# A ternary feed-forward stage and a sparse-expert stage with their element-wise work dealt out anew over VectorE, ScalarE and GpSimd

## The chip, the cores and the metric

One core of one Trainium2 chip runs the whole program in one launch. The metric is device time in microseconds (us), the median of several executions. Five engines take part, each with its own queue of instructions worked off in order: TensorE (PE, and PEld for its weight loads), VectorE (DVE), ScalarE (ACT), GpSimd (POOL) and SyncE (SP), which only issues transfers here. They meet at semaphores: an instruction adds to one when it is done, and another queue waits until the count is reached. While a queue waits, everything behind the waiting instruction waits too.

## The reference, cut to what matters

Two transformer layers over 2048 tokens of width 512. The change touches both feed-forward parts. Layer 0's is ternary, with hidden width 2048:

```python
def bitlinear(x, w):
    xn = layer_norm(x)
    x_hat = clip(xn * 128 / gamma, -128 + eps, 128 - eps) * gamma / 128   # gamma = max|xn| of the row
    w_hat = sign(round(w / (mean|w| + eps))) * mean|w|
    return x_hat @ w_hat.T
h = gelu(bitlinear(x, w_fc))          # 512 -> 2048
y = bitlinear(h, w_proj)              # 2048 -> 512
x = layernorm(x + y)
```

Layer 1's is a mixture of experts: 16 experts of inner width 352, two for each token, and a shared expert:

```python
gu = x @ w_gate_up[e]                 # 512 -> 704
h  = silu(gu[:352]) * gu[352:]
y += combine[t, e] * (h @ w_down[e])  # 352 -> 512
```

## The kernel before

Every fp32 operand of a product goes to TensorE as two f16 numbers: a high part (rounded to f16) and a low part (what the rounding left). A high part is written by ScalarE, a low part by a subtraction after it.

**The order of the work.** In a stage each engine has a list of pairs (lag, function). In step s it calls, in the order of the list, every function with tile t = s - lag. `unrolled` writes all steps out; `run_tiles` writes the first and last steps out and puts the middle into a loop of two steps. So the order of the list is the order in the engine's queue, and the lag says in which step a tile reaches it. Two buffers (t % 2) stand behind nearly every tile.

**The ternary stage** (`ternary_ffn`) goes over 16 tiles of 128 tokens. In a step TensorE does the first product of one tile (`fc`, 32 matmuls in four banks of PSUM), the transposes of the hidden rows of an older one (`ht`, 32 in four turns through two banks), the transposes of a younger one's input (`xt`) and the second product (`proj`, 32 matmuls). ScalarE applies gelu, bank by bank, and writes both high parts (`xhi`, `hhi`). VectorE has the statistics of three normalisations (`bn_stats`), the normalisations themselves (`normalize`), the search for the largest value and the clip (`AbsmaxQuantizer.apply`), and the residual sum. Copies of the transposed hidden rows from PSUM (`evacuate`) are split, two turns to ScalarE and two to VectorE. GpSimd takes roots (`root`) and both low parts (`xlo`, `hlo`).

**The sparse stage** (`sparse_experts`) goes over 48 tiles of 128 token places, each with its expert's weights. For each tile SyncE loads fp32 weights; ScalarE writes their high parts (`gate_hi`, 128x2816; `down_hi`, 128x1024 and 96x512), VectorE the low parts (`gate_lo`, `down_lo`). TensorE does the two halves of the first product (`gate`, `up`), ScalarE a tanh, VectorE two operations to the hidden rows (`swiglu`; its result is `hid`, announced by `h_done`), ScalarE their high part (`hhi`), GpSimd their low part (`hlo`), TensorE the transposes (`tr`), ScalarE their copy (`hevac`), TensorE the second product (`down`), and ScalarE its copy to SBUF (`yevac`). GpSimd also gathers the token rows.

Of the kernel before, what the change touches and what calls it, by code (L numbers as in the profile page):

```python
# [803 lines left out]
def ternary_ffn(nc, m):  # L804


    NB = FF // D
    NK = FF // P
    with Phase(nc, "ffn") as f:
# [24 lines left out]
        with f.block() as block:
            @block.tensor
            def _(pe):
                def xt(t, u):
# [3 lines left out]
                    transpose_parts(pe, ps_x, x2[u], m).then_inc(xt_done, 1)  # L841

                def fc(t, u, banks):
                    pe.wait_ge(xt_evac, t + 1)
                    for n in banks:
                        after(pe, gelu_done, t * NB - (NB - n - 1))
                        for k in range(KC):
                            for part in range(2):
                                last = pe.matmul(ps_fc[n][:, :], xT[u][:, part, k, :],  # L849
                                                 m.wfcT[:, k, n * D:(n + 1) * D],  # L850
                                                 start=(k == 0 and part == 0), stop=(k == KC - 1 and part == 1))
# [2 lines left out]
                def ht(t, u, turns):
                    pe.wait_ge(hh_done, t + 1)
                    pe.wait_ge(hl_done, t + 1)
                    for g in turns:
                        part, k0 = part_of(g)
                        after(pe, (ht_evac_a, ht_evac_d)[g % 2], t * 2 + g // 2)
                        for k in range(8):  # L860
                            last = pe.transpose(ps_h[g % 2][:, k, :],  # L861
                                                h2[u][:, part, (k0 + k) * P:(k0 + k + 1) * P], m.ident16[:, :])
                        last.then_inc(ht_done, 1)

                def proj(t, u):
# [1226 lines left out]
```

## Time and profile before

| | |
|---|---|
| median of 3 runs | 2095.75 us (2095.16 to 2096.2) |
| the profiled execution's own time | 2098.51 us |
| its span | 2096.7 us |
| PE, DVE, ACT, POOL busy, share of the span | 80%, 70%, 48%, 27% |
| mean granted TensorE clock | 0.93 of full speed |
| ternary stage, first and last instruction of VectorE | 774.75 to 1104.4 us |
| sparse stage, first gather to the last copy of a result | 1594.3 to 1975.9 us |

A row of the timeline gives the start of an instruction (or of several merged ones) from the start of the span, its duration, both in us, the engine, the line, what is written and what is read, and in brackets how long its engine sat idle before it and who ended the wait. The distance between two starts on one engine is what an instruction really takes of its queue: it is about 0.1 us shorter than the duration where the next one need not wait for its result. The stages follow each other with a barrier between them, so that time won or lost in one is won or lost for the program unless the next stage has a transfer to wait for.

### The profile page before, as it was taken

How to read it: one execution, taken by the hardware profiler on the slowest of the kernel's cores; microseconds unless marked ns; L12 is line 12 of the kernel's file. 1: busy time of each engine (PE TensorE's matmuls, PEld its weight loads, DVE VectorE, ACT ScalarE, POOL GpSimd, SP SyncE). 2: the span in 40 equal slices, each digit the busy share in tenths (PEclk: the TensorE clock that was granted, in tenths of full speed). 3: DMA queues.
4: the chain of work that ended last, by engine and by line, in shares of the span. 5: the costliest groups of instructions: out<-in, count | busy, mean ns of one | idle time of the engine just before them, and what ended most of it. 6: DMA issues, size and time to landing. Idle time of an engine off the chain costs nothing. (4 is left out here: it accounts for less than half of the span.)

```text
span 2096.7 us, 35409 instructions
## 1 busy us (share of the span) xinstructions
PE 1678.1 (80%) x13401; PEld 864.9 (41%) x13401; DVE 1463.9 (70%) x2115; ACT 997.4 (48%) x1549; POOL 571.1 (27%) x568
## 2 busy tenths in 40 slices
PE   0579999777999858888984977974696888888697
PEld 0353333344333223444441543543463555555364
DVE  3558998446898478999963364364624999999667
ACT  4345777434677713333333222222133777777532
POOL 0250000252000033344321122123261444444255
PEclk9889999998999989999996988996798999999899
DMA  8000000000000000000002000002004665345234
GB/s 298 1 2 2 2 2 2 1 1 1 2 2 2 2 1 1 1 0 0 1 1 91 1 1 1 1 1 96 32 2 144 195 195 153 113 154 183 94 102 139
DMA packets 49393, 105.96 MB, mean 51 GB/s; under 512 B 7096, under 2 KB 10392, under 8 KB 48720
## 3 DMA queue, kind: packets, MB, share of 16 engines
q1 hardware_dynamic: 37632, 75.99, 10.4%
q0 software_dynamic: 7424, 21.00, 3.9%
q10 hardware_dynamic: 4176, 6.82, 0.9%
q8 instruction: 103, 1.69, 0.3%
q14 instruction: 58, 0.48, 0.1%
HBM read 149.68 MB, written 21.01 MB: 81 GB/s over the span
## 5 line engine op out<-in xcount | busy, mean ns | idle before, releaser
L624 ACT ACTIVATE attn_prob<-attn_ps_t 128x512 f32<-128x512 f32 x576 | 312.6, 595 | 127.9 <-PE attn_ps_t L591 126.3
L643 DVE TENSOR_REDUCE attn_mx<-attn_ps_s 128x2 f32<-128x1024 f32 (+3 forms) x304 | 342.8, 1163 | 41.5 <-PE attn_ps_s L572 38.0
L136 PE MATMUL sparse_ps_g<-sparse_wg,sparse_xT 128*128 128x352 f16 x1152 | 190.5, 316 | 54.7 <-DVE sparse_xT L1900 54.7
L604 PE MATMUL attn_ps_o<-attn_prob,V 128*32 128x256 f32 x2304 | 174.8, 389 | 3.6 <-ACT attn_prob L624 2.7
L1905 DVE SCALAR_TENSOR_TENSOR sparse_wg<-sparse_raw_g,sparse_wg 128x2816 f16<-128x2816 f32 x48 | 148.4, 3092 | 37.9 <-ACT sparse_wg L1857 37.8
L136 PEld LDWEIGHTS sparse_ps_g<-sparse_wg,sparse_xT 128*128 128x128 f16 x1152 | 107.8, 99 | 128.8 <-DVE sparse_xT L1900 77.7
L778 POOL TENSOR_TENSOR wo_o<-O,wo_o 128x512 f16<-128x512 f32 (+1 forms) x16 | 18.4, 1153 | 496.0 <-ACT wo_o L750 495.9
L1942 POOL TENSOR_TENSOR sparse_h<-sparse_hid,sparse_h 128x352 f16<-128x352 f32 x48 | 87.7, 1826 | 217.4 <-ACT sparse_h L1876 217.4
L1021 PE MATMUL lin_ps_z<-w,lin_xT 128*128 128x512 f16 x576 | 136.2, 387 | 0.0
L1857 ACT ACTIVATE sparse_wg<-sparse_raw_g 128x2816 f16<-128x2816 f32 x48 | 122.0, 2541 | 17.2 <-DMA sparse_raw_g<-in_L_ffn_w_gate_up_dram 17.2
L849 PE MATMUL ffn_ps_fc<-wfcT,ffn_xT 128*128 128x512 f16 x512 | 123.6, 393 | 8.1 <-DVE ffn_xT L926 8.1
L591 PE MATMUL attn_ps_t<-QT,KT 64*128 64x256 f16 x1152 | 112.3, 273 | 18.6 <-ACT attn_prob L624 11.4
L871 PE MATMUL ffn_ps_y<-wprojT,ffn_hT 128*128 128x512 f16 x512 | 116.2, 386 | 10.6 <-issue 8.8
L572 PE MATMUL attn_ps_s<-KT,QT 64*128 64x512 f16 (+3 forms) x768 | 115.2, 336 | 2.1 <-DVE attn_mx L643 2.1
L1845 PE MATMUL sparse_ps_y<-sparse_wd,sparse_hT 128*128 128x512 f16 (+1 forms) x432 | 102.7, 383 | 1.0 <-ACT sparse_hT L1883 1.0
L908 ACT ACTIVATE ffn_hT<-ffn_ps_h 128x1024 f16<-128x1024 f16 x32 | 32.8, 1024 | 138.2 <-PE ffn_ps_h L861 138.2
L1021 PEld LDWEIGHTS lin_ps_z<-w,lin_xT 128*128 128x128 f16 x576 | 53.3, 99 | 70.3 <-issue 15.6
L591 PEld LDWEIGHTS attn_ps_t<-QT,KT 64*128 64x128 f16 x1152 | 39.0, 94 | 100.0 <-ACT attn_prob L624 45.1
L871 PEld LDWEIGHTS ffn_ps_y<-wprojT,ffn_hT 128*128 128x128 f16 x512 | 50.0, 99 | 71.4 <-issue 14.2
L604 PEld LDWEIGHTS attn_ps_o<-attn_prob,V 128*32 128x32 f32 x2304 | 49.3, 108 | 69.9 <-issue 37.5
L849 PEld LDWEIGHTS ffn_ps_fc<-wfcT,ffn_xT 128*128 128x128 f16 x512 | 49.9, 100 | 65.7 <-DVE ffn_xT L926 8.9
L962 POOL TENSOR_TENSOR ffn_h<-ffn_hn,ffn_h 128x2048 f16<-128x2048 f32 x16 | 65.0, 4065 | 37.4 <-ACT ffn_h L906 37.4
(320 smaller groups left out, 3407.2 us busy)
## 6 DMA issues: line engine op xcount, KB each, us to landing
sparse_raw_g<-in_L_ffn_w_gate_up_dram SPq DMA_DIRECT2D x48, 1408.0 KB
sparse_raw_d<-in_L_ffn_w_down_dram SPq DMA_DIRECT2D x48, 512.0 KB
y_d<-sparse_y SPq DMA_DIRECT2D x48, 256.0 KB, 3.6
sparse_raw_d<-in_L_ffn_w_down_dram SPq DMA_DIRECT2D x48, 192.0 KB
prep_w_fc<-in_L_ffn_w_fc_dram SPq DMA_DIRECT2D x4, 1024.0 KB, 15.6
X<-in_L_attn_x_dram ACTq DMA_DIRECT2D x1, 4096.0 KB, 39.6
prep_w_proj<-in_L_ffn_w_proj_dram SPq DMA_DIRECT2D x4, 1024.0 KB, 22.4
x_d<-route_x SPq DMA_DIRECT2D x16, 256.0 KB, 2.0
```

Of the source, the lines that this page charges most:

```text
L136: last = pe.matmul(out, a(k), b(k), start=(k == 0 and n == 0), stop=(k == chunks - 1 and n == 2))
L572: last = pe.matmul(banks[par][:, h, :], QT[s, pair + h, qt * P:(qt + 1) * P], KT[s, (pair + h) // 2, c * 512:c * 512 + n], start=not diago ...
L591: last = pe.matmul(ps_t[:, (2 * g + par) % 3, i, :], KT[s, j, kt * P:(kt + 1) * P], QT[s, 2 * j:2 * j + 2, qt * P:(qt + 1) * P], start=kt ...
L604: last = pe.matmul(ps_o[32 * jj:32 * jj + 32, 256 * half:256 * half + 256], V[:, kt, 4 * jg + jj, :], prob[(2 * q + jj // 2) % 4][:, half, ...
L624: act.activation(prob[g % 4][:, par, :, :], ps_t[:, (2 * g + par) % 3, :, :], ACT.Exp, scale=HD ** -0.5).then_inc(exp_done, 1)
L643: dve.tensor_reduce(mx[x % 2][:, c, :, at:at + per], ps_s[:, 2 * (r % 2):2 * (r % 2) + 2, 0:per * n].rearrange("p e (h k) -> p e h k", k=n ...
L849: last = pe.matmul(ps_fc[n][:, :], xT[u][:, part, k, :], m.wfcT[:, k, n * D:(n + 1) * D], start=(k == 0 and part == 0), stop=(k == KC - 1 ...
L871: last = pe.matmul(ps_y[:, :], hT[u][:, part, k, :], m.wprojT[:, k, :], start=(k == 0 and part == 0), stop=(k == NK - 1 and part == 1))
L1021: last = pe.matmul(out, xT[:, a, k, :], m.w1[:, b, i, k, :], start=False, stop=(k == KC - 1 and n == 2))
L1845: last = pe.matmul(ps_y[u][:, :], hT[u][0:size, a, k, :], wd[u][0:size, c, k, :], start=(k == 0 and n == 0), stop=(k == 2 and n == 2))
L1857: act.activation(wg[u][:, 0, :, :], raw_g[r][:, :, :], ACT.Copy, scale=WS).then_inc(gh_done, 1)
L1905: dve.scalar_tensor_tensor(wg[u][:, 1, :, :], raw_g[r][:, :, :], WS, wg[u][:, 0, :, :], ALU.mult, ALU.subtract).then_inc(gl_done, 1)
```

## The change

In the ternary stage the loop gives way to steps written out one by one, and the work is dealt out in another way:

- GpSimd keeps the roots, and multiplies the root of the hidden rows by minus their mean (`shift`). Both low parts go to VectorE.
- ScalarE applies the normalisation of the hidden rows (one 128x2048 operation with the root as scale and `shift` as bias) and copies all four turns of transposed rows. VectorE loses these.
- The lags are shorter by one from the hidden normalisation on (`proj` has 6 in place of 7), the lists are in another order, the first transposes of a tile wait for its high part alone, and each half of `proj` waits for its own two turns.

In the sparse stage `hlo` moves from GpSimd to VectorE, between `xevac` and `down_lo`, and on ScalarE `hhi` and `down_hi` change places.

```diff
 @block.tensor                                                    # ternary stage
-                def ht(t, u, turns):
-                    pe.wait_ge(hh_done, t + 1)
-                    pe.wait_ge(hl_done, t + 1)
+                def ht(t, turns):
+                    pe.wait_ge(hh_done, t + 1)
+                    if turns[0] == 2:
+                        pe.wait_ge(hl_done, t + 1)
...
-                    pe.wait_ge(ht_evac_a, t * 2 + 2)
-                    pe.wait_ge(ht_evac_d, t * 2 + 2)
                     for part in range(2):
+                        pe.wait_ge(ht_evac, t * 4 + 2 * part + 2)
...
-                run_tiles(pe, NT, [(4, of(fc, 0)), (7, of(ht, 0, 1)), (4, of(fc, 1, 2)), (7, of(ht, 2, 3)),
-                                   (4, of(fc, 3)), (3, xt), (7, proj)])
+                unrolled(NT, [(4, lambda t: fc(t, (0,))), (6, lambda t: ht(t, (0, 1))), (4, lambda t: fc(t, (1, 2))),
+                              (6, lambda t: ht(t, (2, 3))), (4, lambda t: fc(t, (3,))), (3, xt), (6, proj)])
 @block.scalar
+                def h_norm(t):
+                    u = t % 2
+                    act.wait_ge(shift_done, t + 1)
+                    after(act, hl_done, t - 1)
+                    act.activation(hn[u][:, :], h[u][:, :, :].rearrange("p n k -> p (n k)"), ACT.Identity,
+                                   scale=ln_h.rstd[u][:, :], bias=shift[u][:, :]).then_inc(hn_done, 1)
...
-                run_tiles(act, NT, [(7, evacuate(act, copy, ht_evac_a, 0)), (4, gelu(0, 1)),
-                                    (7, evacuate(act, copy, ht_evac_a, 2)), (4, gelu(2, 3)), (2, xhi), (6, hhi)])
+                unrolled(NT, [(4, gelu(0)), (6, hevac(0, 1)), (5, hhi), (4, gelu(1, 2)), (6, hevac(2, 3)), (4, gelu(3)),
+                              (2, xhi), (4, h_norm)])
 @block.vector
+                    dve.tensor_scalar(back[u][:, :], ln_h.mv[u][:, 0:1], -1.0, None, ALU.mult).then_inc(back_done, 1)
+                def h_clip(t):
+                    dve.wait_ge(hn_done, t + 1)
+                    q_h.apply(dve, hn[t % 2][:, :], t, t % 2)
+                def hlo(t):
+                    u = t % 2
+                    dve.wait_ge(hh_done, t + 1)
+                    after(dve, ht_done, t * 4 - 4)
+                    dve.tensor_tensor(h2[u][:, 1, :], hn[u][:, :], h2[u][:, 0, :], ALU.subtract).then_inc(hl_done, 1)
...
-                run_tiles(dve, NT, [(6, h_norm), (9, norm), (8, residual), (7, turn(1)), (5, h_stats), (7, turn(3)),
-                                    (3, x_evac), (1, x_norm), (0, x_stats)])
+                unrolled(NT, [(5, h_clip), (8, norm), (7, residual), (5, hlo), (1, x_norm), (4, h_stats), (3, x_evac), (2, xlo), (0, x_stats)])
 @block.gpsimd
+                def h_root(t):
+                    u = t % 2
+                    after(pool, hn_done, t - 1)
+                    pool.wait_ge(ln_h.s_var, t + 1)
+                    pool.tensor_tensor(ln_h.rstd[u][:, :], ln_h.var[u][:, :], m.minus_half[:, :], ALU.pow).then_inc(ln_h.s_rstd, 1)
+                    pool.wait_ge(back_done, t + 1)
+                    pool.wait_ge(ln_h.s_rstd, t + 1)
+                    pool.tensor_tensor(shift[u][:, :], back[u][:, :], ln_h.rstd[u][:, :], ALU.mult).then_inc(shift_done, 1)
...
-                run_tiles(pool, NT, [(8, lambda t, u: ln_r.root(pool, t, u)), (5, lambda t, u: ln_h.root(pool, t, u)),
-                                     (6, hlo), (2, xlo), (0, lambda t, u: ln_x.root(pool, t, u))])
+                unrolled(NT, [(7, lambda t: ln_r.root(pool, t, t % 2)), (4, h_root), (0, lambda t: ln_x.root(pool, t, t % 2))])
 sparse stage
-                unrolled(NG, [(1, gate_hi), (2, tanh), (3, hevac), (2, down_hi), (2, hhi), (3, yevac)])
+                unrolled(NG, [(1, gate_hi), (2, tanh), (3, hevac), (2, hhi), (2, down_hi), (3, yevac)])
...
-                unrolled(NG, [(1, gate_lo), (2, swiglu), (1, xevac), (2, down_lo)])
+                unrolled(NG, [(1, gate_lo), (2, swiglu), (1, xevac), (2, hlo), (2, down_lo)])
...
-                unrolled(NG, [(0, gather), (2, hlo)])
+                unrolled(NG, [(0, gather)])
```

Three places show what this does to a queue. The first is ScalarE in the middle of the sparse stage, before the change, from one high part of the hidden rows (`sparse_h`) to the next; `sparse_y` is `yevac`, `sparse_wg` is `gate_hi`, `sparse_th` the tanh, `sparse_hT` is `hevac` and `sparse_wd` is `down_hi`:

```order
L1876 ACTIVATE sparse_h<-sparse_hid 128x352
L1889 ACTIVATE sparse_y<-sparse_ps_y 128x512
L1857 ACTIVATE sparse_wg<-sparse_raw_g 128x2816
L1870 ACTIVATE sparse_th<-sparse_ps_g 128x352
L1882 ACTIVATE sparse_hT<-sparse_ps_h 128x2x256
L1883 ACTIVATE sparse_hT<-sparse_ps_h 96x2x128
L1863 ACTIVATE sparse_wd<-sparse_raw_d 128x1024
L1864 ACTIVATE sparse_wd<-sparse_raw_d 96x512
L1876 ACTIVATE sparse_h<-sparse_hid 128x352
```

And ScalarE at the same place after the change; the lines have other numbers, since functions ahead of them have grown:

```order
L1896 ACTIVATE sparse_h<-sparse_hid 128x352
L1883 ACTIVATE sparse_wd<-sparse_raw_d 128x1024
L1884 ACTIVATE sparse_wd<-sparse_raw_d 96x512
L1909 ACTIVATE sparse_y<-sparse_ps_y 128x512
L1877 ACTIVATE sparse_wg<-sparse_raw_g 128x2816
L1890 ACTIVATE sparse_th<-sparse_ps_g 128x352
L1902 ACTIVATE sparse_hT<-sparse_ps_h 128x2x256
L1903 ACTIVATE sparse_hT<-sparse_ps_h 96x2x128
L1896 ACTIVATE sparse_h<-sparse_hid 128x352
```

`down_hi` stood ahead of the high part of the hidden rows, and now stands between it and `yevac` with the next `gate_hi`.

The second place is VectorE in a full step of the ternary stage, before the change, from the normalisation of the hidden rows (`ffn_hn`) to their statistics:

```order
L717 TENSOR_SCALAR ffn_hn<-ffn_h,ffn_lnh_mv,ffn_lnh_rstd 128x2048
L794 TENSOR_REDUCE ffn_qh_g<-ffn_hn 128x1
L797 TENSOR_SCALAR ffn_qh_limit<-ffn_qh_g 128x1 x2
L800 TENSOR_SCALAR ffn_hn<-ffn_hn,ffn_qh_limit 128x2048
L717 TENSOR_SCALAR X<-ffn_r,ffn_lnr_mv,ffn_lnr_rstd 128x512
L940 SCALAR_TENSOR_TENSOR ffn_r<-ffn_ps_y,gamma,X 128x512
L700 BN_STATS ffn_lnr_stats<-ffn_r 128x6
L703 MEMSET ffn_lnr_pad 128x1
L704 BN_AGGR ffn_lnr_mv<-ffn_lnr_stats 128x2
L706 TENSOR_SCALAR ffn_lnr_var<-ffn_lnr_mv 128x1
L885 COPY ffn_hT<-ffn_ps_h 128x1024
L700 BN_STATS ffn_lnh_stats<-ffn_h 128x6 x4
```

And VectorE after the change, from the search for the largest value (the first operation of `h_clip`) to the normalisation of the next input (`ffn_xn`):

```order
L794 TENSOR_REDUCE ffn_qh_g<-ffn_hn 128x1
L797 TENSOR_SCALAR ffn_qh_limit<-ffn_qh_g 128x1 x2
L800 TENSOR_SCALAR ffn_hn<-ffn_hn,ffn_qh_limit 128x2048
L717 TENSOR_SCALAR X<-ffn_r,ffn_lnr_mv,ffn_lnr_rstd 128x512
L965 SCALAR_TENSOR_TENSOR ffn_r<-ffn_ps_y,gamma,X 128x512
L700 BN_STATS ffn_lnr_stats<-ffn_r 128x6
L703 MEMSET ffn_lnr_pad 128x1
L704 BN_AGGR ffn_lnr_mv<-ffn_lnr_stats 128x2
L706 TENSOR_SCALAR ffn_lnr_var<-ffn_lnr_mv 128x1
L960 TENSOR_TENSOR ffn_h<-ffn_hn,ffn_h 128x2048
L717 TENSOR_SCALAR ffn_xn<-X,ffn_lnx_mv,ffn_lnx_rstd 128x512
```

The normalisation in front is gone, and so is the copy of transposed rows (`ffn_hT`) behind the residual's statistics; in the copy's place stands the low part of the hidden rows (`ffn_h`, a subtraction over 2048 columns), and the statistics of the hidden rows now come after the input's normalisation and clip.

## Rows read from the trace of the kernel before

**Rows 1.** Busy time by engine, granted clock and DMA in the middle of both stages.
```profile
880.00:970.00 90.00, 76.23 (x477) 39.45 (x476) 86.17 (x145) 32.88 (x38) 33.84 (x23) 0.98 0.00 0
1720.00:1820.00 100.00, 85.52 (x616) 50.23 (x615) 93.10 (x82) 78.75 (x107) 40.37 (x27) 1.00 0.45 134
```

**Rows 2.** Timeline of the sparse stage, one tile's round.
```profile
1780.66 0.52 DVE L1915 SCALAR_TENSOR_TENSOR sparse_hid<-sparse_a,sparse_ps_g 128x352 f32<-128x352 f32 x1
...
1781.21 0.50 ACT L1876 ACTIVATE sparse_h<-sparse_hid 128x352 f16<-128x352 f32 x1 [1.58 <-DVE sparse_hid L1915]
...
1781.79 1.84 POOL L1942 TENSOR_TENSOR sparse_h<-sparse_hid,sparse_h 128x352 f16<-128x352 f32 x1 [4.34 <-ACT sparse_h L1876]
...
1782.10 2.54 ACT L1857 ACTIVATE sparse_wg<-sparse_raw_g 128x2816 f16<-128x2816 f32 x1
1782.83 1.34 DVE L1923 SCALAR_TENSOR_TENSOR sparse_wd<-sparse_raw_d,sparse_wd 96x512 f16<-96x512 f32 x1
...
1784.67 3.09 DVE L1905 SCALAR_TENSOR_TENSOR sparse_wg<-sparse_raw_g,sparse_wg 128x2816 f16<-128x2816 f32 x1 [0.49 <-ACT sparse_wg L1857]
...
1785.62 1.06 ACT L1863 ACTIVATE sparse_wd<-sparse_raw_d 128x1024 f16<-128x1024 f32 x1
...
1786.57 0.63 ACT L1864 ACTIVATE sparse_wd<-sparse_raw_d 96x512 f16<-96x512 f32 x1
...
1788.23 0.52 DVE L1915 SCALAR_TENSOR_TENSOR sparse_hid<-sparse_a,sparse_ps_g 128x352 f32<-128x352 f32 x1
```

**Rows 3.** The shape of `down_lo`'s last piece, behind the sparse stage, by shape.
```profile
L1531 DVE SCALAR_TENSOR_TENSOR ws_d<-sparse_raw_d,ws_d 96x512 f16<-96x512 f32 x1 | 0.7, 679 | 0.0
```

**Rows 4.** Timeline of the ternary stage, VectorE and GpSimd.
```profile
942.97 2.46 DVE L700 BATCH_NORM_STATS2 ffn_lnh_stats<-ffn_h 128x6 f32<-128x512 f32 x4
...
945.76 0.15 DVE L706 TENSOR_SCALAR ffn_lnh_var<-ffn_lnh_mv 128x1 f32<-128x1 f32 x1
...
947.07 0.54 DVE L717 TENSOR_SCALAR ffn_xn<-X,ffn_lnx_mv,ffn_lnx_rstd 128x512 f32 x1
...
948.61 4.40 DVE L800 TENSOR_SCALAR ffn_xn<-ffn_xn,ffn_qx_limit 128x512 f32<-128x512 f32 x1
948.66 4.07 POOL L962 TENSOR_TENSOR ffn_h<-ffn_hn,ffn_h 128x2048 f16<-128x2048 f32 x1 [2.11 <-ACT ffn_h L906]
...
955.86 2.29 DVE L794 TENSOR_REDUCE ffn_qh_g<-ffn_hn 128x1 f32<-128x2048 f32 x1
...
959.69 0.54 DVE L717 TENSOR_SCALAR X<-ffn_r,ffn_lnr_mv,ffn_lnr_rstd 128x512 f32 x1
...
961.99 0.69 DVE L885 COPY ffn_hT<-ffn_ps_h 128x1024 f16<-128x1024 f16 x1
```

**Rows 5.** Timeline of the ternary stage, TensorE: first product, one round, last product.
```profile
784.87 8.42 PE L849 MATMUL ffn_ps_fc<-wfcT,ffn_xT 128*128 128x512 f16 x32 [2.34 <-DVE ffn_xT L926]
...
946.65 7.07 PE L871 MATMUL ffn_ps_y<-wprojT,ffn_hT 128*128 128x512 f16 x32 [0.75 <-issue]
...
962.74 0.62 PE L861 MATMUL ffn_ps_h<-ident,ffn_h 128*128 128x128 f16 x8 [2.50 <-DVE ffn_hT L885]
...
966.29 7.07 PE L871 MATMUL ffn_ps_y<-wprojT,ffn_hT 128*128 128x512 f16 x32 [0.75 <-issue]
...
1094.21 7.07 PE L871 MATMUL ffn_ps_y<-wprojT,ffn_hT 128*128 128x512 f16 x32 [0.90 <-ACT ffn_hT L908]
```

**Rows 6.** Groups of like instructions by shape, nearest to those the change adds.
```profile
L906 ACT ACTIVATE ffn_h<-ffn_hn 128x2048 f16<-128x2048 f32 x16 | 30.4, 1900 | 0.0
L908 ACT ACTIVATE ffn_hT<-ffn_ps_h 128x1024 f16<-128x1024 f16 x32 | 32.8, 1024 | 138.2 <-PE ffn_ps_h L861 138.2
L711 POOL TENSOR_TENSOR ffn_lnh_rstd<-ffn_lnh_var,minus_half 128x1 f32<-128x1 f32 x16 | 8.8, 548 | 54.1 <-DVE ffn_lnh_var L706 54.1
L1008 DVE SCALAR_TENSOR_TENSOR w<-linw_rawWqk,w 128x2048 f16<-128x2048 f32 x1 | 2.3, 2293 | 10.5 <-ACT w L1000 10.5
L411 POOL TENSOR_TENSOR qkv_pad<-minus_half 128x1 f32<-128x1 f32 x16 | 3.1, 193 | 1.3
```

More of the change, by code:

```diff
@@ L817, in ternary_ffn @@
         r = [f.sb(f"r{u}", [P, D], F32) for u in range(2)]
+        back = [f.sb(f"back{u}", [P, 1], F32) for u in range(2)]
+        shift = [f.sb(f"shift{u}", [P, 1], F32) for u in range(2)]
+        ps_fc = [f.ps(f"ps_fc{n}", [P, D], F32) for n in range(NB)]
         ps_x = f.ps("ps_x", [P, 2, KC, P], F16)
-        ps_fc = [f.ps(f"ps_fc{n}", [P, D], F32) for n in range(NB)]
         ps_h = [f.ps(f"ps_h{n}", [P, 8, P], F16) for n in range(2)]
@@ L840, in xt, with fc @@
                     after(pe, xt_evac, t)
-                    transpose_parts(pe, ps_x, x2[u], m).then_inc(xt_done, 1)
-                def fc(t, u, banks):
+                    transpose_parts(pe, ps_x, x2[t % 2], m).then_inc(xt_done, 1)
+                def ht(t, turns):
+                    pe.wait_ge(hh_done, t + 1)
+                    if turns[0] == 2:
+                        pe.wait_ge(hl_done, t + 1)
+                    for g in turns:
+                        after(pe, ht_evac, t * 4 + g - 1)
+                        part, k0 = g // 2, (g % 2) * 8
+                        for k in range(8):
+                            last = pe.transpose(ps_h[g % 2][:, k, :],
+                                                h2[t % 2][:, part, (k0 + k) * P:(k0 + k + 1) * P], m.ident16[:, :])
+                        last.then_inc(ht_done, 1)
+                def fc(t, banks):
+                    u = t % 2
                     pe.wait_ge(xt_evac, t + 1)
@@ L848, in fc, with proj @@
                             for part in range(2):
[L849 to L850 removed]
+                                last = pe.matmul(ps_fc[n][:, :], xT[u][:, part, k, :], m.wfcT[:, k, n * D:(n + 1) * D],
                                                  start=(k == 0 and part == 0), stop=(k == KC - 1 and part == 1))
                         last.then_inc(fc_done, 1)
[L854 to L867 removed]
+                def proj(t):
+                    u = t % 2
                     after(pe, r_done, t)
                     for part in range(2):
+                        pe.wait_ge(ht_evac, t * 4 + 2 * part + 2)
                         for k in range(NK):
@@ L908, in _, with hhi @@
-                copy = lambda out, in_: act.activation(out, in_, ACT.Copy)
-                run_tiles(act, NT, [(7, evacuate(act, copy, ht_evac_a, 0)), (4, gelu(0, 1)),
-                                    (7, evacuate(act, copy, ht_evac_a, 2)), (4, gelu(2, 3)), (2, xhi), (6, hhi)])
+                def hhi(t):
+                    u = t % 2
+                    act.wait_ge(q_h.s_clipped, t + 1)
+                    after(act, ht_done, t * 4 - 6)
+                    act.activation(h2[u][:, 0, :], hn[u][:, :], ACT.Copy).then_inc(hh_done, 1)
```

101 lines of the change are left out of this document (46 added, 55 removed).

## The prediction

> **What bounds the kernel now.** I read the busy time by stretch first, to see which engine is full in the two stages, and then one round (one tile's share) of each in the timeline, to see which wait ends last.
>
> In the ternary stage VectorE is busy 86.17 of 90 us and TensorE 76.23 [rows 1]. TensorE waits 2.50 us for VectorE's copy of transposed rows, and 0.75 us more ahead of `proj`; its round is 966.29 - 946.65 = 19.64 us [rows 5]. VectorE sets it, and not by work alone: the clip of the input (128x512) takes 4.40 us, and ends when GpSimd's low part of 4.07 us, begun 0.05 us later, has ended [rows 4]. A normalisation of the same shape takes 0.54 [rows 4], so 3.9 us a round are a lock-out.
>
> In the sparse stage VectorE is busy 93.10 of 100 us, and DMA 0.45 [rows 1]. Here the timeline is needed, for VectorE still waits 0.49 us for ScalarE in every round. The round is a ring through two engines [rows 2]: `hid` starts at 1780.66; ScalarE, idle for 1.58 us, starts the high part 0.55 later; with `yevac` between them `gate_hi` starts 0.89 after that; `gate_lo` 2.57 after it; the next `hid` 3.56 after it. The sum is 7.57 us. Whatever ScalarE does between the wait for `hid` and `gate_hi` lengthens the ring; what it does ahead of the wait is covered by 1.58 us of idleness. `down_hi` is now ahead of it.
>
> **The change, part by part: the sparse stage.** `down_hi` goes behind the high part, into the ring. Its first piece holds ScalarE's queue for 1786.57 - 1785.62 = 0.95 us, its second for about 0.53 (0.63 less the overlap of 0.1) [rows 2]. The ring becomes 7.57 + 1.48 = 9.05 us. What lay under cover ahead of `hid` leaves only more idleness there.
>
> VectorE gains a subtraction over 352 columns, about 0.5 us (its neighbour of that width takes 0.52) [rows 2]. Its input is ready 0.55 + 0.50 us after `hid` starts; VectorE has until then its `hid` and the copy of `xT` (0.69 for that shape [rows 4]), so it hardly waits. VectorE loses a stall: `down_lo`'s last piece takes 1.34 us while GpSimd's low part runs [rows 2], and 0.68 with GpSimd quiet [rows 3]. VectorE's own work was 7.57 - 0.49 = 7.08 and becomes 7.08 - 0.66 + 0.5 = 6.9 us, far under 9.05: nothing is won. `down_lo` waits for `down_hi`, until 2.5 us after `hid`, and is through 1.8 us later, before `gate_lo` may start at 5.5. TensorE has 0.86 x 7.57 = 6.5 us of work [rows 1] and stays covered. The transfers have more time than before.
>
> The ring is closed from tile 0's `hid` to tile 46's: 46 rounds, 46 x 1.48 = 68 us, and about 0.4 at the end, where tile 47's second product waits for `down_lo`. **Sparse stage: +68.5.** Bounds: with the pieces' whole durations, 1.06 + 0.63 = 1.69, it is 78; if the second piece overlapped with its successor as the first does, by 0.11, 67.
>
> **The ternary stage.** GpSimd's two subtractions go, and with them the 3.9 us. I sum VectorE's round after the change from the start of `h_clip` in its new order. Largest value, limits and clip: 959.69 - 955.86 = 3.83; output normalisation, residual and its statistics: 961.99 - 959.69 = 2.30; low part of 2048 columns: 2.2, from the same subtraction of weights at 2.29 less overlap [rows 4, 6]; input normalisation, largest value and clip: 948.61 - 947.07 = 1.54 plus 0.46 for the clip; hidden statistics to the start of the variance: 945.76 - 942.97 = 2.79 [rows 4]. That makes 13.12 us.
>
> Then the root. GpSimd starts 0.25 us after the variance has started and takes 0.55 [rows 6]. The new multiplication (`shift`, 128x1) could start at 0.85. VectorE meanwhile clears the copy of `xT` and starts `xlo` at about 0.8, for 0.68 (the row of this width) [rows 3]. The rows show that such a subtraction and a GpSimd operation exclude each other: GpSimd's 1.84 us began when VectorE's piece ran, VectorE's 1.34 waited for the end of it [rows 2]. So I let the multiplication wait until 1.46 and take 0.2, as a 128x1 operation of 0.193 does [rows 6]. ScalarE's normalisation of 2048 columns takes 1.90, as its high part does [rows 6], and 0.1 goes to signals. `h_clip` can start 3.66 after the variance. **Round: 13.12 + 3.66 = 16.8 us.** Without the collision it is 16.2.
>
> The Trainium skill (SBUF — State Buffer, Who interferes with whom) says the same of the pair: a VectorE instruction with two inputs in SBUF contends with a GpSimd one that reads SBUF, whichever starts first holding it off. It speaks against `xlo` beside `shift`; by it the round is the longer of my two, and the rows of the sparse stage agree (1.34 us against 0.68).
>
> The other engines: TensorE's round is 19.64 - 2.50 - 0.75 = 16.4 us [rows 5], just covered. ScalarE adds 1.90 and two copies of 1.02 [rows 6] to the 32.88 us that it has in 90 [rows 1]: about 11 us, covered as a sum, but in the order of its queue the high part of the hidden rows stands behind two copies. It is ready for it 3.97 us after `h_clip` starts, and VectorE asks for it at 6.13; 1.9 us fit between.
>
> The edges. The copy of the first `xT` now stands behind one more input normalisation and `xlo`, so the first `fc` starts about 2.5 us later than 784.87 [rows 5], at 787.4. It takes 8.4; gelu 0.9; statistics 2.79; to `h_clip` 3.66: 803.1. There the pipe is not yet full, and `h_clip` (3.9), high part (2.0), low part (2.2), input (2.0), statistics (2.79) and root path (3.66) stand in a line: `h_clip` of tile 1 at 819.7. 14 rounds of 16.8 less about 2 for the last three, which have no input work, give 1053 for tile 15. There ScalarE does the copies of tile 14's second half only behind tile 15's high part, at 7.9; half a `proj` later, at 11.4, tile 15's transposes and copies take 3.1 and its `proj` 7.07: end at 1053 + 21.6 = 1074.6, against 1094.21 + 7.07 = 1101.3 [rows 5]. **Ternary stage: -27.** Bounds: a round of 16.2 gives -35; a round of 17.5 (if the low part were 0.3 slower, and half a microsecond went to signals) gives -17. The vanished loop I cost at nothing, for the 0.75 us of TensorE in the round is within the time that it has to spare.
>
> **The sum.** 2098.5 (the profiled execution) + 68.5 - 27 = 2140; the median lies 2.75 lower, so 2137 us.
>
> **The rivals.**
> (1) The forecast: the sparse ring grows by 1.48, the ternary round lies between 16.2 and 17.5. From 2095.75 + 67 - 35 to + 78 - 17: 2128 to 2157. Chance 0.76.
> (2) The ternary stage gains little, because ScalarE becomes the place where it queues: copies wait for TensorE, the high part behind them, and with it VectorE's low part. For: the order of its queue, in which one late copy holds up four functions. Against: 2.2 us of room ahead of the high part. It decides when TensorE's first transposes come more than about 2 us late; a round of 18.5 gives 14 x 1.7 = 24 us back: 2161. Chance 0.11.
> (3) The sparse stage doesn't grow, and the whole is faster: if `gate_hi` were ready well ahead of need, the 1.48 us would fall into idle time, and the ternary gain would stand alone: 2095.75 - 27 = 2069. It takes 1.48 us of slack between `gate_hi`'s end and `gate_lo`. Against: the slack is negative, 0.49 us of waiting in every round, and `gate_lo` starts 0.03 after `gate_hi` has ended [rows 2]. Chance 0.05.
> (4) A mixture near no change: half of the sparse loss (34) and a ternary gain of 35, about 2096. Nothing in the rows would halve the loss. Chance 0.03.
> (5) TensorE, idle longer in the sparse stage, is granted less clock: it has 1.00 there with 0.86 busy and 0.98 in the ternary stage [rows 1]; its share falls to 0.72. Only if its work rose beyond the ring would it count; 0.3 us a round are 14 us: 2151. Chance 0.05, inside the range.
>
> **The numbers.** The likeliest is 2137. Below 2120 lie (3), (4) and an edge of (1), above 2155 lies (2) and a little of (1): 2120 to 2155 leaves out about 0.2. A measurement of this kernel can tell 0.2%, 4.2 us, from no change. Faster by more has (3) and a third of (4): 0.06; within it 0.02; slower 0.92.
>
> **What would show each step.** The sparse rounds at 9.05 us, `down_hi` between the high part and `yevac`, ScalarE's idleness ahead of `hid` up from 1.58 to about 3.1 and VectorE's ahead of `gate_lo` from 0.49 to about 1.3; `down_lo`'s last piece at 0.68. In the ternary stage no 128x512 clip over 0.6, rounds of 16.8, `shift` starting when `xlo` ends, VectorE idle for ScalarE's normalisation about 1.2 us a round. Rounds of 7.6 in the sparse stage would refute the ring; ternary rounds over 17.5 would refute the order that I summed, and a `shift` that starts beside `xlo` the collision.

## The result: 2138.74 us, and the profile after

The changed kernel takes 2138.74 us, the median of four runs (2135.87 to 2142.16); the kernel before took 2095.45 beside it (2093.37 to 2096.2, four runs). The ratio is 1.0209 with an interval of 1.0187 to 1.023: 43.3 us more. The forecast was 2137, with 2120 to 2155 as its range. The profiled execution took 2135.87 us with a span of 2134.1, against 2098.51 and 2096.7 before.

The busy time in the same stretches as in [rows 1] (length; PE, PEld, DVE, ACT and POOL busy; the granted clock; DMA share and GB/s):

```profile
880.00:970.00 90.00, 87.44 (x558) 45.11 (x557) 80.87 (x165) 54.13 (x56) 22.56 (x23) 1.00 0.00 1
1720.00:1820.00 100.00, 73.24 (x518) 43.28 (x519) 77.19 (x79) 66.53 (x90) 37.34 (x11) 1.00 0.38 124
```

The two stages went opposite ways. In the ternary stage TensorE rose from 76.23 to 87.44 of 90 us: the same work is packed closer. In the sparse stage every engine fell, VectorE from 93.10 to 77.19 of 100 and TensorE from 85.52 to 73.24, and so did the DMA: all of them wait.

One round of the sparse stage after the change, from the timeline (start, duration, engine, line, operation, names, and in brackets the idle time before it and what ended it). It answers to [rows 2]:

```profile
1800.72 0.52 DVE L1935 SCALAR_TENSOR_TENSOR sparse_hid<-sparse_a,sparse_ps_g 128x352 f32<-128x352 f32 x1
...
1801.27 0.50 ACT L1896 ACTIVATE sparse_h<-sparse_hid 128x352 f16<-128x352 f32 x1 [3.04 <-DVE sparse_hid L1935]
1801.67 1.04 ACT L1883 ACTIVATE sparse_wd<-sparse_raw_d 128x1024 f16<-128x1024 f32 x1
1801.80 0.53 DVE L1950 TENSOR_TENSOR sparse_h<-sparse_hid,sparse_h 128x352 f16<-128x352 f32 x1
...
1802.62 0.61 ACT L1884 ACTIVATE sparse_wd<-sparse_raw_d 96x512 f16<-96x512 f32 x1
...
1803.14 0.57 ACT L1909 ACTIVATE sparse_y<-sparse_ps_y 128x512 f32<-128x512 f32 x1
1803.26 1.23 DVE L1941 SCALAR_TENSOR_TENSOR sparse_wd<-sparse_raw_d,sparse_wd 128x1024 f16<-128x1024 f32 x1 [0.94 <-ACT sparse_wd L1884]
...
1803.62 2.54 ACT L1877 ACTIVATE sparse_wg<-sparse_raw_g 128x2816 f16<-128x2816 f32 x1
...
1804.41 0.68 DVE L1943 SCALAR_TENSOR_TENSOR sparse_wd<-sparse_raw_d,sparse_wd 96x512 f16<-96x512 f32 x1
...
1806.18 3.09 DVE L1925 SCALAR_TENSOR_TENSOR sparse_wg<-sparse_raw_g,sparse_wg 128x2816 f16<-128x2816 f32 x1 [1.10 <-ACT sparse_wg L1877]
...
1806.70 3.40 POOL L1961 DMA_INDIRECT sparse_xg<-x_d,token  x1 [5.63 <-PE sparse_ps_x L1830]
...
1809.74 0.52 DVE L1935 SCALAR_TENSOR_TENSOR sparse_hid<-sparse_a,sparse_ps_g 128x352 f32<-128x352 f32 x1
```

`hid` to `hid` is 1809.74 - 1800.72 = 9.02 us, where it was 7.57. Follow it with a finger: `hid` ends the 3.04 us wait of ScalarE, the high part starts 0.55 after it, `down_hi` takes 1803.14 - 1801.67 = 1.47, then `yevac` and `gate_hi`, which ends VectorE's wait of 1.10; `gate_lo`, and `hid` again. The waits over 300 us of the stage say the same (waiting engine, tile, line, what it waited for; sum, times, longest):

```profile
ACT sparse_h L1896 <- DVE sparse_hid L1935: 100.4, 33, 3.0
...
DVE sparse_wg L1925 <- ACT sparse_wg L1877: 36.2, 33, 1.1
```

Two engines that wait for each other in every round are a ring; neither is full.

One round of the ternary stage after the change, VectorE, GpSimd and ScalarE; it answers to [rows 4]:

```profile
943.05 2.29 DVE L960 TENSOR_TENSOR ffn_h<-ffn_hn,ffn_h 128x2048 f16<-128x2048 f32 x1
943.20 2.63 POOL L711 TENSOR_TENSOR ffn_lnr_rstd<-ffn_lnr_var,minus_half 128x1 f32<-128x1 f32 x1 [6.81 <-DVE ffn_lnr_var L706]
...
946.81 0.55 DVE L800 TENSOR_SCALAR ffn_xn<-ffn_xn,ffn_qx_limit 128x512 f32<-128x512 f32 x1
...
950.07 0.15 DVE L706 TENSOR_SCALAR ffn_lnh_var<-ffn_lnh_mv 128x1 f32<-128x1 f32 x1
...
950.80 0.68 DVE L938 TENSOR_TENSOR ffn_x<-ffn_xn,ffn_x 128x512 f16<-128x512 f32 x1
...
951.06 0.47 POOL L984 TENSOR_TENSOR ffn_shift<-ffn_back,ffn_lnh_rstd 128x1 f32<-128x1 f32 x1
...
951.57 2.09 ACT L907 ACTIVATE ffn_hn<-ffn_h,ffn_shift,ffn_lnh_rstd 128x2048 f32<-128x2048 f32 x1 [4.67 <-POOL ffn_shift L984]
...
953.69 2.29 DVE L794 TENSOR_REDUCE ffn_qh_g<-ffn_hn 128x1 f32<-128x2048 f32 x1 [1.20 <-ACT ffn_hn L907]
...
966.80 0.15 DVE L706 TENSOR_SCALAR ffn_lnh_var<-ffn_lnh_mv 128x1 f32<-128x1 f32 x1
...
970.42 2.29 DVE L794 TENSOR_REDUCE ffn_qh_g<-ffn_hn 128x1 f32<-128x2048 f32 x1 [1.20 <-ACT ffn_hn L907]
```

The clip of the input takes 0.55 where it took 4.40. The round is 970.42 - 953.69 = 16.73 us, where TensorE's was 19.64 [rows 5]. That round of before was one of the longer ones: in the middle of the stage the starts of VectorE's search for the largest hidden value (the first operation of `h_clip`) lay 18.5 to 20.1 us apart. From the first of these starts to the last the stage took 267.4 us before (807.1 to 1074.5) and takes 247.3 now. The last product of the stage:

```profile
1068.47 7.07 PE L875 MATMUL ffn_ps_y<-wprojT,ffn_hT 128*128 128x512 f16 x32
```

It ends at 1075.54, against 1101.28 [rows 5]. So the ternary stage is 25.7 us shorter by its end (20.1 of them between the first and the last search), and the sparse one 67.2 us longer (first to last `hid`: 1584.5 to 2004.7 after, 1614.7 to 1967.7 before).

### The profile page after: what moved, and what is told of

It is laid out like the page before. It is cut to its first block and busy times, and to the rows that moved or that the text cites. A ratio compares the mean times of both kernels' runs of the same rounds, so it can differ in the third digit from the quotient of the medians.

```text
span 2134.1 us, 35297 instructions
## 1 busy us (share of the span) xinstructions
PE 1678.9 (79%) x13401; PEld 868.7 (41%) x13401; DVE 1411.1 (66%) x2163; ACT 1055.3 (49%) x1597; POOL 515.6 (24%) x504
## 5 line engine op out<-in xcount | busy, mean ns | idle before, releaser
L1961 POOL DMA_INDIRECT sparse_xg<-x_d,token x48 | 152.7, 3182 | 275.1 <-PE sparse_ps_x L1830 264.6
L591 PE MATMUL attn_ps_t<-QT,KT 64*128 64x256 f16 x1152 | 112.3, 273 | 18.5 <-ACT attn_prob L624 11.4
L1896 ACT ACTIVATE sparse_h<-sparse_hid 128x352 f16<-128x352 f32 x48 | 23.8, 496 | 144.1 <-DVE sparse_hid L1935 144.1
L1941 DVE SCALAR_TENSOR_TENSOR sparse_wd<-sparse_raw_d,sparse_wd 128x1024 f16<-128x1024 f32 x48 | 58.8, 1226 | 45.2 <-ACT sparse_wd L1884 45.2
L1865 PEld LDWEIGHTS sparse_ps_y<-sparse_wd,sparse_hT 128*128 128x128 f16 (+1 forms) x432 | 38.6, 98 | 90.8 <-ACT sparse_hT L1903 50.3
```

The costliest lines, as they stand in the source:

```text
L591: last = pe.matmul(ps_t[:, (2 * g + par) % 3, i, :], KT[s, j, kt * P:(kt + 1) * P], QT[s, 2 * j:2 * j + 2, qt * P:(qt + 1) * P], start=kt ...
L1865: last = pe.matmul(ps_y[u][:, :], hT[u][0:size, a, k, :], wd[u][0:size, c, k, :], start=(k == 0 and n == 0), stop=(k == 2 and n == 2))
L1961: pool.indirect_dma_start(xg[u][:, :], None, m.x2_d, bass.IndirectOffsetOnAxis(ap=m.token[:, g:g + 1], axis=0)).then_inc(x_in[u], 16)
```

## The experiments

### Each half by itself

`e1_ternary_alone` is the kernel before with the new ternary function; `e2_sparse_alone` the kernel before with the new sparse lists.

```diff
 e1: ternary_ffn() as after the change, sparse_experts() as before
 e2: ternary_ffn() as before, sparse_experts() as after the change
```

> The ternary stage of the change with the sparse stage of before. My theory: the two stages add up, and the ternary one is worth what the profile of the changed kernel shows between its first and last VectorE instruction, 303.2 us against 329.1: -26 us, so about 2069 to 2070 us, a ratio of 0.987. Rival: the two parts work on each other (code loading, the clock, the addresses of buffers), and the sum of this run's and the next one's differences misses the +43 of the change by over 6 us.

> The sparse stage of the change with the ternary stage of before. My theory (the ring through ScalarE grows by down_hi): rounds of 9.02 to 9.05 us, +67 to +69 us, about 2163 us, a ratio of 1.032. Rival (both parts work on each other): anything under +60.

Measured: e1 2070.52 us (2069.31 to 2074.86), ratio 0.9889 [0.9872, 0.9905]; e2 2164.24 us (2162.23 to 2164.91), ratio 1.033 [1.0313, 1.0348]; the kernel before 2095.31 beside both. That is -24.8 and +68.9, in sum +44.1, where the whole change measured +43.3. The halves add, and the change holds a gain that its other half hides.

### Which of the two sparse edits costs

`e3_low_part_moved` moves only `hlo` to VectorE; `e8_high_part_first` exchanges only the two functions on ScalarE and leaves `hlo` on GpSimd.

```diff
 e3, VectorE and GpSimd
-                unrolled(NG, [(1, gate_lo), (2, swiglu), (1, xevac), (2, down_lo)])
+                unrolled(NG, [(1, gate_lo), (2, swiglu), (1, xevac), (2, hlo), (2, down_lo)])
-                unrolled(NG, [(0, gather), (2, hlo)])
+                unrolled(NG, [(0, gather)])
 e8, ScalarE
-                unrolled(NG, [(1, gate_hi), (2, tanh), (3, hevac), (2, down_hi), (2, hhi), (3, yevac)])
+                unrolled(NG, [(1, gate_hi), (2, tanh), (3, hevac), (2, hhi), (2, down_hi), (3, yevac)])
```

> Of the sparse change only the low part's move from GpSimd to VectorE; ScalarE's order is that of before. My theory: the ring through hid, high part, yevac, gate_hi and gate_lo is as long as before, VectorE loses a stall of 0.66 us and gains an operation of 0.52 under it, rounds stay at 7.57 us and the time within 0.2% of before. Rival (the loss comes from VectorE taking work in a stage in which it is busy 93 of 100 us): rounds of 7.57 + 0.5, +24 us or more, up to the whole +67.

> Of the sparse change only the exchange of two names in ScalarE's list: hhi ahead of down_hi; the low part stays on GpSimd. My theory: the whole loss is here, rounds of 9.0 to 9.05 us and +66 to +69 us (about 2163). GpSimd still collides with VectorE, but beside idle time. Rival (VectorE's added work is the cause): no change.

Measured: e3 2095.31 us (ten runs, 2094.43 to 2099.45), ratio 1.0002 [0.9993, 1.0012]; e8 2163.53 us (2163.28 to 2164.52), ratio 1.0327 [1.031, 1.0345]. The whole loss, 68.2 of e2's 68.9 us, is the one exchange of two names in ScalarE's list. From e8's timeline:

```profile
1776.01 0.52 DVE L1915 SCALAR_TENSOR_TENSOR sparse_hid<-sparse_a,sparse_ps_g 128x352 f32<-128x352 f32 x1
...
1776.57 0.50 ACT L1876 ACTIVATE sparse_h<-sparse_hid 128x352 f16<-128x352 f32 x1 [3.04 <-DVE sparse_hid L1915]
...
1777.14 0.86 POOL L1942 TENSOR_TENSOR sparse_h<-sparse_hid,sparse_h 128x352 f16<-128x352 f32 x1 [7.06 <-ACT sparse_h L1876]
...
1785.04 0.52 DVE L1915 SCALAR_TENSOR_TENSOR sparse_hid<-sparse_a,sparse_ps_g 128x352 f32<-128x352 f32 x1
```

The round is 9.03 us, with the low part on GpSimd as before. And from e3's:

```profile
1779.74 0.52 DVE L1915 SCALAR_TENSOR_TENSOR sparse_hid<-sparse_a,sparse_ps_g 128x352 f32<-128x352 f32 x1
...
1782.40 0.68 DVE L1923 SCALAR_TENSOR_TENSOR sparse_wd<-sparse_raw_d,sparse_wd 96x512 f16<-96x512 f32 x1
...
1783.75 3.09 DVE L1905 SCALAR_TENSOR_TENSOR sparse_wg<-sparse_raw_g,sparse_wg 128x2816 f16<-128x2816 f32 x1 [0.67 <-ACT sparse_wg L1857]
...
1787.30 0.52 DVE L1915 SCALAR_TENSOR_TENSOR sparse_hid<-sparse_a,sparse_ps_g 128x352 f32<-128x352 f32 x1
```

The move frees `down_lo`'s piece (0.68 where it was 1.34) and lets VectorE wait 0.67 instead of 0.49; the round stays at 7.56. Work that an engine saves inside a ring which it doesn't fill turns into waiting.

### What in the ternary stage gives the gain

`e4_loop_written_out` is the kernel before with only the ternary loop written out step by step, on all four engines, lists and lags as they were.

```diff
-                run_tiles(dve, NT, [(6, h_norm), (9, norm), (8, residual), (7, turn(1)), (5, h_stats), (7, turn(3)),
+                unrolled_u(NT, [(6, h_norm), (9, norm), (8, residual), (7, turn(1)), (5, h_stats), (7, turn(3)),
```

> The kernel of before with the ternary stage's loop of two steps written out, split and order untouched. My theory: the round of 19 us is VectorE's with its lock-out, the loop's cost lies under it, the time stays within 0.2% of before. Rival (the unrolling is a good part of the gain of 26 us): the 0.75 us that TensorE idles ahead of proj go and with them 10 us or more.

Measured: 2096.08 us (ten runs, 2090.78 to 2098.69), ratio 1.0001 [0.9992, 1.0011]. In the time the loop was worth nothing. In the trace the rounds have become even (18.98 us) and the fifteen from the first to the last search take 264.8 us against 267.4, so up to 2.6 us may be the loop's; the spread of the runs hides that much. TensorE's idle time ahead of `proj`, which the rival would have had gone, is there as before (0.73 us). And so is the lock-out (the sixteen clips of the input; shortest, median and longest in ns):

```profile
L805 DVE TENSOR_SCALAR ffn_xn<-ffn_xn,ffn_qx_limit x16: 545/4327/4427, 776.4 to 1002.3; 128x512 f32<-128x512 f32 x16
```

`e6_hidden_low_gpsimd` is e1 with the low part of the hidden rows back on GpSimd, so that the suspect alone returns.

```diff
-                unrolled(NT, [(5, h_clip), (8, norm), (7, residual), (5, hlo), (1, x_norm), (4, h_stats), (3, x_evac), (2, xlo), (0, x_stats)])
+                unrolled(NT, [(5, h_clip), (8, norm), (7, residual), (1, x_norm), (4, h_stats), (3, x_evac), (2, xlo), (0, x_stats)])
-                unrolled(NT, [(7, lambda t: ln_r.root(pool, t, t % 2)), (4, h_root), (0, lambda t: ln_x.root(pool, t, t % 2))])
+                unrolled(NT, [(7, lambda t: ln_r.root(pool, t, t % 2)), (5, hlo), (4, h_root), (0, lambda t: ln_x.root(pool, t, t % 2))])
```

> The ternary stage of the change (sparse stage of before) with the hidden rows' low part back on GpSimd. My theory (the exclusion of the two engines, not VectorE's own work, made the old round long): 128x512 operations of 4 to 4.5 us come back on VectorE, and although VectorE has 2.2 us less to do a round, rounds grow from 16.7 to about 18.2, +20 us against the ternary stage alone, about 2091. Rival (VectorE's share of work sets the round): VectorE is relieved, rounds fall to TensorE's 16.1 to 16.4, -5 us or more.

Measured: 2076.87 us (2073.63 to 2078.12), ratio 0.9906 [0.989, 0.9923] to 2094.68 beside it. The lock-out is back:

```profile
910.12 4.07 POOL L984 TENSOR_TENSOR ffn_h<-ffn_hn,ffn_h 128x2048 f16<-128x2048 f32 x1
...
910.75 3.72 DVE L800 TENSOR_SCALAR ffn_xn<-ffn_xn,ffn_qx_limit 128x512 f32<-128x512 f32 x1
```

The clip starts inside GpSimd's 4.07 us and ends 0.28 after it (914.47 against 914.19). But it costs only some 6 us against e1 (the intervals of the two runs overlap, so the size rests on the trace), not the 20 that I had expected: the lock-out adds 3.72 - 0.55 = 3.2 us a round, and VectorE is rid of a subtraction of 2.29, so a round is 17.71 against 16.73 in the middle, and over the fifteen rounds from the first to the last `h_clip` 6.4 us are lost (253.7 against 247.3). The direction of the theory held; its size did not, because I had priced the cover and not what moves away with it.

So the low part's move is worth 6.4 of the 20 us that these fifteen rounds gained, and most of the gain is there with the lock-out still in place (253.7 against 267.4, or against e4's 264.8). No run takes the other moves one by one; what follows is an estimate from the rows of e4 and e6. In e4 VectorE does without a wait what e6 has moved to ScalarE:

```profile
920.10 0.69 DVE L890 COPY ffn_hT<-ffn_ps_h 128x1024 f16<-128x1024 f16 x1
920.71 2.46 DVE L705 BATCH_NORM_STATS2 ffn_lnh_stats<-ffn_h 128x6 f32<-128x512 f32 x4
...
931.60 1.35 DVE L722 TENSOR_SCALAR ffn_hn<-ffn_h,ffn_lnh_mv,ffn_lnh_rstd 128x2048 f32<-128x2048 f32 x1
932.99 2.29 DVE L799 TENSOR_REDUCE ffn_qh_g<-ffn_hn 128x1 f32<-128x2048 f32 x1
```

The normalisation is 932.99 - 931.60 = 1.39 us of its queue and each of the two copies 0.61, together 2.6; the stalled clip is 0.6 shorter in e6; against that VectorE has `xlo` (0.6) and waits some 1.3 for ScalarE's normalisation. That is 1.3 us less a round, and the rounds went from 18.98 to 17.71. What the shorter lags and the earlier transposes have part in this stays open.

### The collision of `shift` and the low part of the input

`e5_low_after_stats` is e1 with the input's statistics ahead of its low part, so that no subtraction runs when GpSimd computes `shift`.

```diff
-                unrolled(NT, [(5, h_clip), (8, norm), (7, residual), (5, hlo), (1, x_norm), (4, h_stats), (3, x_evac), (2, xlo), (0, x_stats)])
+                unrolled(NT, [(5, h_clip), (8, norm), (7, residual), (5, hlo), (1, x_norm), (4, h_stats), (3, x_evac), (0, x_stats), (2, xlo)])
```

> The ternary stage of the change (sparse stage of before) with the input's low part behind the input's statistics in VectorE's list, so that no subtraction runs when GpSimd multiplies by the root. My theory: shift takes 0.19 us every time in place of 0.47 to 0.54, ScalarE's normalisation starts 0.3 to 0.35 earlier, rounds fall from 16.73 to about 16.4 and the time by 4 to 5 us against the run with the ternary stage alone (2070.5). Rival (the ring is not VectorE and its return path, but TensorE, which is busy 97% there): rounds stay.

Measured: 2067.96 us (2064.75 to 2069.39), ratio 0.9867 [0.985, 0.9883]. Its interval overlaps that of e1, so the time alone doesn't tell. The trace does:

```profile
914.27 0.15 DVE L706 TENSOR_SCALAR ffn_lnh_var<-ffn_lnh_mv 128x1 f32<-128x1 f32 x1
...
915.26 0.19 POOL L984 TENSOR_TENSOR ffn_shift<-ffn_back,ffn_lnh_rstd 128x1 f32<-128x1 f32 x1
...
917.61 2.29 DVE L794 TENSOR_REDUCE ffn_qh_g<-ffn_hn 128x1 f32<-128x2048 f32 x1 [0.90 <-ACT ffn_hn L907]
```

`shift` takes 0.19 instead of 0.47, VectorE's wait falls from 1.20 to 0.90, and first to last `h_clip` takes 244.4 us instead of 247.3, so 2.9 where I had expected 4 to 5. More isn't to be had: TensorE is busy 209.04 of 210 us between 820 and 1030.

### The ring opened

`e7_ring_opened` keeps the new ternary stage and the sparse low part on VectorE, and gives the sparse lists another order: ScalarE prepares `down_hi` and `gate_hi` ahead of its wait for `hid`. On VectorE `down_lo` comes ahead of `hlo`; `gate_lo` with lag 0 at the end of the list is the same place in the queue as with lag 1 at its start. `e10_ring_alone` is the sparse stage of e7 with the ternary stage of before; `e9_both_orders` is e7 with e5's exchange.

```diff
 ScalarE
-                unrolled(NG, [(1, gate_hi), (2, tanh), (3, hevac), (2, hhi), (2, down_hi), (3, yevac)])
+                unrolled(NG, [(2, tanh), (3, hevac), (2, down_hi), (0, gate_hi), (2, hhi), (3, yevac)])
 VectorE
-                unrolled(NG, [(1, gate_lo), (2, swiglu), (1, xevac), (2, hlo), (2, down_lo)])
+                unrolled(NG, [(2, swiglu), (1, xevac), (2, down_lo), (2, hlo), (0, gate_lo)])
```

> The ternary stage of the change, and a sparse stage whose ring is opened: on ScalarE gate_hi of a tile comes ahead of hhi of the tile two before it, on VectorE the low part of the hidden rows behind down_lo. My theory: the wait for hid no longer stands ahead of gate_hi, the round becomes VectorE's own work of 6.9 us or TensorE's of about 7.1, 46 rounds x 0.45 = 21 us under the ternary stage alone: about 2049. Rival (gate_hi must wait for TensorE's second half in its new place, or the high part is late for the transposes): rounds stay at 7.57 or grow.

> The kernel before with the sparse stage of e7_ring_opened alone (both low parts on VectorE, and ScalarE's work for gate_hi ahead of the wait for hid); the ternary stage is the kernel before's. Theory (in the sparse stage the ring alone sets the round, VectorE's own work comes next): the sparse part of e7_ring_opened's gain stands alone. Its 47 rounds took 322.2 us where the same stage took 352.8 with the old order, so 30.6 us less: 2095 - 30.6 = 2064. Rival (part of that gain came from the new ternary stage, by transfers or by the start of the stage): over 2070.

> e7_ring_opened with the one exchange of e5_low_after_stats in the ternary stage: the statistics of the input ahead of its low part in VectorE's order, so that GpSimd's shift finds VectorE in no two-input subtraction. Theory (the collision of shift and the low part costs 0.3 us a round and TensorE's 16.3 us a round bounds what is won): 2040.1 - 2.6 = 2037.5, the ternary rounds 16.4. Rival (the two orders don't add, or the exchange was worth nothing): 2040 or more.

Measured: e7 2040.09 us (2039.28 to 2041.61), ratio 0.9736 [0.972, 0.9752] to 2094.68; e10 2068.27 (2066.93 to 2069.45), ratio 0.9865 [0.9847, 0.9882] to 2096.14; e9 2039.25 (2037.32 to 2041.0), ratio 0.9725 [0.9708, 0.9743]. From e7's timeline, and its busy time in the same stretch of the sparse stage as above:

```profile
1747.31 2.54 ACT L1877 ACTIVATE sparse_wg<-sparse_raw_g 128x2816 f16<-128x2816 f32 x1
...
1747.94 0.52 DVE L1935 SCALAR_TENSOR_TENSOR sparse_hid<-sparse_a,sparse_ps_g 128x352 f32<-128x352 f32 x1
...
1751.15 3.08 DVE L1925 SCALAR_TENSOR_TENSOR sparse_wg<-sparse_raw_g,sparse_wg 128x2816 f16<-128x2816 f32 x1
...
1754.70 0.52 DVE L1935 SCALAR_TENSOR_TENSOR sparse_hid<-sparse_a,sparse_ps_g 128x352 f32<-128x352 f32 x1
```

```profile
1720.00:1820.00 100.00, 96.26 (x691) 56.26 (x689) 98.91 (x106) 89.52 (x117) 14.11 (x15) 1.00 0.51 164
```

`gate_hi` ends at 1749.85, 1.3 us before `gate_lo` starts without a wait; the round is 6.76 us with VectorE busy 98.91 of 100 and TensorE 96.26. Now work is the bound and not the ring. I had expected 2049, from TensorE's work of about 7.1 us a round; that was too high, and the gain is 9 us larger. e10's stage, first to last `hid`, takes 1939.6 - 1615.9 = 323.7 us where it was 353.0, so 29.3 are gained where the theory had 30.6; the median shows 27.9 and stays under the rival's 2070. So the sparse half pays by itself. It differs from the kernel before in two things, `gate_hi` ahead of the wait and `hlo` on VectorE behind `down_lo`; the second alone, in the old order, was worth nothing (e3), but e10 has not been run with `hlo` on GpSimd. Its gain and e1's add up: 27.9 + 24.8 = 52.7, against e7's 54.6. e7 is the best version together with e9. That e9 adds to it isn't shown: its ternary stage is 2.9 us shorter as e5's was (244.4 against 247.3), and its median 0.84, inside the spread.

## Why the prediction was right

**The ring.** It grew by 1.45 us (7.57 to 9.02), forecast 1.48: `down_hi`'s pieces hold the queue for 0.95 and 0.52 us. Over the 47 rounds between the 48 starts of `hid`, 420.2 against 353.0 us, +67.2, forecast +68.5; e8 shows that no other edit has part in it. ScalarE's wait ahead of the high part is 3.04 (forecast 3.1), `down_lo`'s last piece 0.68 as forecast, VectorE's wait ahead of `gate_lo` 1.10 where I said 1.3. The prediction's own terms give 5.5 - 2.5 - 1.8 = 1.2, for it had `down_lo` wait for `down_hi` (0.94 in the row) and be through 4.3 us after `hid`; it was through after 4.37. The lower bound of this term is off by a little too: 46 x 1.47 = 67.6, and the 0.4 at the end was left out of it.

**The ternary round.** 16.73, forecast 16.8. From `h_clip` to the variance 966.80 - 953.69 = 13.11, forecast 13.12. From the variance to the next `h_clip` 3.62, forecast 3.66, but two terms were off and cancelled. ScalarE's normalisation takes 2.09 and not 1.90: I had priced it by an operation that stores f16 and has no scale and bias. `shift` does not wait to 1.46 and then take 0.2: it starts at 951.06, beside the low part, takes 0.47 and ends at 951.53, when that has ended (950.80 + 0.68 = 951.48). So "`shift` starting when `xlo` ends" was wrong as a row and right as a mechanism; the collision costs 0.28 us a round (e5) where I gave it 0.6. The Trainium skill (SBUF — State Buffer, Who interferes with whom) has such a pair exclude each other; the rows agree, 0.47 against e5's 0.19. I had written that a `shift` which starts beside `xlo` would refute the collision. It does start beside it, and the collision is there all the same: that sign was a bad one, for here the row of the operation that is held off begins while the other still runs (0.47 us in place of 0.19).

**The edges.** First `h_clip` at 803.69 and second at 820.23, forecast 803.1 and 819.7. The last is at 1050.99, forecast 1053: three rounds of 15.6 to 15.9 at the end and three of 16.54 at the start, where I had taken off 2 us in all. From there to the end of the last product I said 21.6 us, and it took 24.5. The term that was short is the product of tile 14, which I took at the 7.07 of the others. It took 9.45 (and so it did before the change, 9.47 from 1069.43 on, which the sum had passed over). That is 2.4 of the missing 2.9; the rest is that it starts 5.1 us after the last `h_clip`, when VectorE's residual has read the bank, and the sum needed about 4.4. TensorE had been idle ahead of it and its granted clock had fallen (the row of the product, then busy times with the columns of the section on the result):

```profile
1056.08 9.45 PE L875 MATMUL ffn_ps_y<-wprojT,ffn_hT 128*128 128x512 f16 x32 [2.63 <-DVE ffn_r L965]
...
1050.00:1056.00 6.00, 1.23 (x16) 0.91 (x16) 4.93 (x6) 3.84 (x4) 0.00 (x0) 0.84 0.00 0
1056.00:1061.00 5.00, 4.92 (x12) 1.79 (x13) 3.81 (x7) 2.68 (x3) 2.54 (x1) 0.51 0.02 5
1061.00:1066.00 5.00, 5.00 (x33) 2.58 (x32) 0.42 (x1) 0.00 (x0) 0.00 (x0) 1.00 0.00 0
```

Behind six microseconds with 1.23 busy the clock is at its lower level for five (0.51 of full speed, 1.2 GHz), and they hold 12 matmuls where the next five hold 33. The end came at 1075.54, forecast 1074.6: -25.7 against before, forecast -27. That it is so near is in part luck, for the rounds were 2 us shorter and the end 2.9 longer than forecast. e1 by itself measured -24.8.

**The sum.** The two profiled executions differ by 2135.87 - 2098.51 = 37.4 us, where the two stages give 67.2 - 25.7 = 41.5. The missing 4 us lie between them, in stages that no edit touches: from the bias operation (the 1x2048 subtraction behind the ternary stage) to the first `hid` 484.4 us after and 489.2 before. Over all profiled executions of this study that stretch takes 484.4 to 491.1 us, whatever the edit, so I count it as scatter; what makes it was not tried and stays open. The same scatter is the reason why e5's and e9's 2.9 us don't stand out of their times.

The forecast took over from the kernel before that the median lies 2.75 under the profiled execution; after the change it lies 2.87 above it. So 2137 against 2138.74 is nearer than the runs allow one to claim: what is borne out is the sum of the stages, 67.2 - 25.7 = 41.5 against 68.5 - 27 = 41.5, and in this sum too the two misses, 1.3 us each, cancel.

**The rivals.** (2) asked for copies on ScalarE that come late and a round of 18.5; it is 16.73. (3) needed slack ahead of `gate_lo`; e8 refutes it. (4) is refuted by e1 and e2, each at nearly its full size. (5) asked for a lower clock in the sparse stage; it stays at 1.00 with TensorE busy 73.24 of 100.

## What to carry to other kernels

Where two in-order queues wait for each other once in a round, draw the ring and sum it: an instruction costs its whole time if it stands between a wait of the ring and the signal that closes it, and nothing if it stands ahead of the wait under idle time. Here one exchange of neighbours cost 68 us, and another order (with the low part on VectorE) won 29. Look for that order before moving work between engines, and time the halves of a change apart, for a gain of 25 us lay under this loss. When a suspect is moved back to price it, count also what its engine gets rid of.

## What was not expected of the hardware

The gather of tokens on GpSimd (`DMA_INDIRECT`) takes 3.40 us in the round shown above, 1.24 in the round of [rows 2], and 0.94 in e7. In the changed kernel it starts at 1806.70, 0.52 after `gate_lo`, and ends at 1810.10, 0.83 after `gate_lo` has (1809.27). In e3 it starts later inside `gate_lo` and ends just as long behind it:

```profile
1776.18 3.09 DVE L1905 SCALAR_TENSOR_TENSOR sparse_wg<-sparse_raw_g,sparse_wg 128x2816 f16<-128x2816 f32 x1 [0.67 <-ACT sparse_wg L1857]
...
1778.16 1.93 POOL L1941 DMA_INDIRECT sparse_xg<-x_d,token  x1 [5.63 <-PE sparse_ps_x L1810]
```

1780.09 is 0.82 after 1779.27. In the round of before it starts inside `down_lo`'s last piece and ends 0.85 after that (1785.02 against 1784.17):

```profile
1783.78 1.24 POOL L1935 DMA_INDIRECT sparse_xg<-x_d,token  x1
```

In e7 it starts 0.07 after `gate_lo` has ended and takes 0.94. So in these three rounds an operation with two inputs on VectorE holds off GpSimd's issue of a gather, not only its arithmetic. The reverse is not seen: in e8 `down_lo`'s first piece starts 0.42 us into a gather, and takes 1.23 us (1.22 in e3) while the gather takes 0.97. It costs nothing here, since the gather is off the ring; a kernel whose gather is late could pay up to 3.40 - 0.94 = 2.5 us a round, which is an estimate.

A root of 128x1 on GpSimd takes 2.63 us beside VectorE's subtraction of 2048 columns, and 0.55 alone [rows 6]: it ends at 945.83, 0.49 after the subtraction. It too is off the path here.

ScalarE's operation with a scale and a bias for each partition takes 2.09 us for 128x2048 where the copy to f16 takes 1.91. Which of the two differences, operands or output type, makes the 0.18 was not tried.
